# Gated cross-attention and FFN on one core: order of the first chunk, reciprocal in halves, a second buffer for the left-over values

## The chip, the cores and the metric

The kernel runs on one core of one Trainium2 chip. The metric is the device time of one execution in microseconds (us), lower is better. The engines are TensorE (PE: matmuls; PEld: its weight loads), VectorE (DVE), ScalarE (ACT), GpSimd (POOL) and SyncE (SP), which here only issues DMAs.

## The reference

Four batches of 2048 tokens with 512 features attend to 154 context rows each, then pass an FFN with a hidden layer of 2048. What is computed:

```python
x = x + tanh(g_xattn[0]) * xattn(layernorm(x), ctx)     # q, k, v, 16 heads of 32, softmax, Wo, bo
x = x + tanh(g_ffn[0]) * ffn(layernorm(x))
# ffn: h = relu(x @ w1.T + b1); hq, wq = fp8(4,3) of h and w2; out = fp16-like(hq @ wq.T + fp16-like(b2))
```

x is (4, 2048, 512) float32, w1 (2048, 512), w2 (512, 2048).

## The kernel before

The 8192 tokens are cut into 16 chunks of 512 tokens (4 tiles of 128). Four chunks belong to one batch. Products that need more than float16 are made of two float16 parts each (high and low) in three passes; the first chunk's q and all k and v are made in float32 directly. Every weight in parts is scaled by a power of two taken from its largest magnitude: `magnitude` reduces a weight to a column of `mag`, `fold` brings the columns together over the partitions, `powers` makes the scales.

The order of all work is written out by hand in **beats**. A chunk c starts at beat 28c; lists such as `VALUE_AT` or `O_AT` give the beats of each stage relative to that, and every engine runs the same loop over beats in its own program, calling the stages that are due. Engines meet through semaphores. Because stages reach from beat -40 to 69, chunk c's attention runs beside the projection, hidden layer and FFN output of chunk c-1. For chunk 0 there is no such work beside it.

Per chunk: `ln1_stat`/`ln1_apply` (VectorE), `x_hi` (ScalarE) and `x_lo` (GpSimd) split x, `turn_x` (SP, L299) transposes both parts by DMA into `xT`; `query` (PE), `query_out`, `query_hi`, `query_lo`; `q_stack` (SP, 12 DMAs a pair). `rank` (PE, L502) makes scores for the row maximum into `m_ps`, `row_max` (DVE, L861) reduces them; one `rank` waits for the `row_max` before it. `shift` and `shift_row` bring the maxima into the stacked q. `lift_left` and `lift_main` (PE) make the shifted scores in `s_ps`, `exps` (ACT) and `probs` (GpSimd) the probabilities in two parts. Of 154 context rows 128 are the main part; the left-over 26 of four heads are laid block by block into `vblk` (`values_diagonal`, SP, L356), once a batch. `value` (PE, L542) sums the probabilities into `d_ps` and the weighted values into `y_ps`; `normalise` (DVE, L878) takes the reciprocal of `d_ps` into `y32` and multiplies by `y_ps`. Then `project` (PE) with `residual` (DVE, with `resid` loaded again from x by `reload`, SP, and `add_bias`, GpSimd), `ln2_inverse` (GpSimd), `ln2_apply` (DVE, into `xn2`), `x2_hi`, `x2_lo`, `turn_x2` (SP, L307) into `late_a`, `hidden` and `relu`, `ffn_out` (PE, L591) and `finish` (DVE, L890: `ffn16`, then the sum into `resid`), `store`. The ring of two PSUM banks serves q, projection, hidden layer and FFN output in order; a job waits until the job two places before it has been read.

Each batch change (chunks 4, 8, 12) also loads `kblk` (`keys_diagonal`) and `kcat` (`keys_stacked`) anew, and `vblk`, which waits for the last `value` of the batch before, because there is one buffer:

```python
if b:
    sp.wait_ge(valued, b * CPB * KT)      # values_diagonal, VBLK_AT = [1]
...
nc.vector.reciprocal(y32[:], d_ps[:]).then_inc(inverted, 1)      # normalise, VALUE_AT
nc.vector.tensor_tensor(y32[:], y_ps[:], y32[:], ALU.mult).then_inc(y_scaled, 1)
```

The beginning (before the loop over beats) loads x, the context, wk, wv, wq and the small arrays on SP's queue, wo and three quarters of w1 on ScalarE's queue once x is turned (`move_turned`); VectorE makes the magnitudes and folds them (`kv_scales`), moves the first four k and v products, folds again with wq (`q_scales`) and moves the first q through the one buffer `q32`; ScalarE casts, GpSimd subtracts.

Of the kernel before, what the change touches and what calls it, by code (L numbers as in the profile page):

```python
# [25 lines left out]
STACK = 3  # L26
PASSES = ((0, 0), (0, 1), (1, 0))
# [5 lines left out]
Q_LOG, K_LOG = 10, 12  # L33

# [43 lines left out]
def build(nc, x, ctx_t, g_xattn, g_ffn, wq_t, bq, wk_t, bk, wv_t, bv, wo_t, bo, w1_t, b1, w2_t, b2, out):  # L78
# [10 lines left out]
    with ExitStack() as es:  # L89
# [17 lines left out]
        vblk = sb("vblk", [P, 2, KT, P], F16)  # L107
# [37 lines left out]
        fold_b = sb("fold_b", [P, 8], F32)  # L145
        amax = sb("amax", [P, 32], F32)
# [65 lines left out]
        kv_done, kv_moved, kv_hi, kv_lo = sem("kv_done"), sem("kv_moved"), sem("kv_hi"), sem("kv_lo")  # L212
        wo_hi_done, wo_ready, w1_hi, w1_ready, w2_ready = (
# [7 lines left out]
        def run(stage_fn, at, b):  # L221

            for k, r in enumerate(at):
                c, rest = divmod(b - r, PERIOD)
                if rest == 0 and 0 <= c < NCH:
                    stage_fn(c, k)

# [41 lines left out]

        def kv32(n):  # L270
            return kv_stage[:, n % 2 * C:(n % 2 + 1) * C]
# [19 lines left out]
        def _(sp):  # L291
# [7 lines left out]
            def turn_x(c, t):  # L299
                sp.wait_ge(x_split, (c - 1) * TILES + t + 1)  # L300
                if t == 0:
                    sp.wait_ge(q_done, c * KT)
                for part in range(2):
# [3 lines left out]
            def turn_x2(c, t):  # L307
                sp.wait_ge(x2_split, c * TILES + t + 1)
# [4 lines left out]
                for part in range(2):  # L313
# [24 lines left out]
            def keys_diagonal(b, k):  # L338
                if b:
                    sp.wait_ge(scored, b * CPB * 16)  # L340
                else:
                    sp.wait_ge(kv_hi, KT)
                    sp.wait_ge(cleared, 1)
# [12 lines left out]
            def values_diagonal(b, k):  # L356
                if b:
                    sp.wait_ge(valued, b * CPB * KT)
                else:
                    sp.wait_ge(kv_lo, KT + 1)  # L360
                for h in range(GH):
                    for a in range(2):
                        sp.dma_start(vblk[DH * h:DH * h + LEFT, a, :, DH * h:DH * h + DH],  # L363
# [41 lines left out]
            for beat in range(FIRST, (NCH - 1) * PERIOD + LAST):  # L405
                run(shift_row, SHIFT_AT, beat)
                run(lambda c, t: x_load(c, t) if c > 1 else None, XLOAD_AT, beat)
                run(turn_x2, X2TURN_AT, beat)
                run(lambda c, t: turn_x(c, t) if c else None, XTURN_AT, beat)
# [13 lines left out]
        def _(pe):  # L423
# [118 lines left out]
            def value(c, m):  # L542
                g, b = group(c, m), c // CPB
                pe.wait_ge(prob_lo, unit(c, m, GH) + 1)
                if g:
                    pe.wait_ge(inverted, g)
# [13 lines left out]
                if g:  # L560
                    pe.wait_ge(y_scaled, g)
                for p, (a, q) in enumerate(PASSES):
# [4 lines left out]
                    for h in range(GH):  # L567
                        last = pe.matmul(y_ps[DH * h:DH * h + DH, :], vblk[:, a, m, DH * h:DH * h + DH],  # L568
# [32 lines left out]

            for n in range(KT):
                turn(n)
# [4 lines left out]
            for beat in range(FIRST, (NCH - 1) * PERIOD + LAST):  # L608
# [3 lines left out]
                run(rank, MAX_AT, beat)  # L612
# [7 lines left out]
        def _(act):  # L620
# [13 lines left out]
            def wq_hi_part():  # L634
# [15 lines left out]
            def first_keys_stacked(pair):  # L650
                act.wait_ge(cleared, 1)
# [59 lines left out]
            def query_hi(c, m):  # L711
# [18 lines left out]
            nc.scalar.activation(sc[:, 8:10], gates[:], ACT.Tanh).then_inc(gate_done, 1)  # L730
            for n in range(KT):
# [4 lines left out]
            wq_hi_part()  # L736
            first_keys_stacked(1)
            w1_load(2)
            for beat in range(FIRST, (NCH - 1) * PERIOD + LAST):
# [7 lines left out]
                run(lambda c, t: x_hi(c, t) if c else None, XSPLIT_AT, beat)  # L747
                once(wo_hi, WO_HI, beat)
# [4 lines left out]
        def _(dve):  # L753
# [11 lines left out]
            def fold():  # L765

                link(nc.vector.transpose(fold_a[:], mag[:]))
# [53 lines left out]
            def o_w1_scales(n):  # L821
                fold()
                powers(pw[:, 3:8], rp[:, 3:8], amax[:, 7:12])
                dve.wait_ge(gate_done, 1)
                nc.vector.tensor_scalar(sc[:, 10:11], rp[:, 3:4], 2.0 ** 7, None, ALU.mult)
# [299 lines left out]
```

## Time and profile before

| what | value |
|---|---|
| time, median of 3 runs | 1725.39 us (1722.44 to 1725.61) |
| the profiled execution | 1727.09 us, its span 1725.3 us |
| PE busy | 1590.5 us, 92% |
| VectorE busy | 935.5 us, 54% |
| GpSimd busy | 864.4 us, 50% |
| ScalarE busy | 804.5 us, 47% |
| mean granted clock of PE | 0.966 |
| DMA, 127.3 MB | 74 GB/s on average |

The profile comes from one execution. The page cuts the span into 40 slices: PE's busy digit is 6, 6, 7, 5, 6 in the first five and mostly 9 after that, and the granted clock (PEclk, 1.0 is 2.4 GHz) shows an 8 and a 6 among the first five slices and a 9 or 8 later. The chain that ended last is PE for 74%, VectorE for 13% and SP's queue for 5%.

### The profile page before, as it was taken

What the parts mean: (1) busy time and instruction counts of PE and PEld (TensorE: products, weight loads), DVE (VectorE), ACT (ScalarE), POOL (GpSimd) and SP (SyncE); (2) the same over time, 40 slices, a digit from 0 to 9 for tenths busy, and PEclk for the clock granted to TensorE, in tenths of its full rate; (3) what the DMA queues carried; (4) which work ended last, traced back from release to release, by engine and by line L of the source; (5) the groups of instructions that cost most, each with busy time, mean ns of one, the idle gap of its engine ahead of it and who ended that gap; (6) DMA issues with size and microseconds to landing.
All of it is one profiled execution on the core that took longest, in us unless ns stands there. A gap on an engine that the chain in (4) does not pass through costs nothing.

```text
span 1725.3 us, 24606 instructions
## 1 busy us (share of the span) xinstructions
PE 1590.5 (92%) x9320; PEld 719.0 (42%) x9320; DVE 935.5 (54%) x1190; ACT 804.5 (47%) x1177; POOL 864.4 (50%) x918
## 2 busy tenths in 40 slices
PE   6675699999899999999979999999979999999998
PEld 3231244444334444444434444444434444444443
DVE  7767557464355746464554746455554645646131
ACT  1354563544345355444525545454534545453511
POOL 2457556473444647364444736465453646535420
PEclk9896899999999999999989999999999999999999
DMA  7322243132222313233231323323232322222010
GB/s 276 76 73 73 68 116 99 36 79 80 68 74 60 101 33 82 71 77 79 63 92 32 81 74 74 74 74 83 53 67 73 77 70 75 56 62 74 0 50 25
DMA packets 216293, 127.30 MB, mean 74 GB/s; under 512 B 164976, under 2 KB 189552, under 8 KB 214512
## 3 DMA queue, kind: packets, MB, share of 16 engines
q1 hardware_dynamic: 213536, 120.01, 27.1%
q10 hardware_dynamic: 2640, 5.72, 0.9%
q8 instruction: 74, 1.21, 0.3%
q14 instruction: 43, 0.35, 0.1%
HBM read 48.20 MB, written 16.78 MB: 38 GB/s over the span
## 4 chain that ended last, share of the span: by engine, by line
PE 74%; DVE 13%; SPq 5%; issue 4%; POOL 2%; DMA 1%; ACT 1%; ACTq 0%; DVEq 0%
PE ring L428 47%; PE ring L598 14%; DVE y L885 3%; PE m_ps L512 3%; PE s_ps L539 2%; PE y_ps L565 2%; DVE resid L925 2%; PE y_ps L568 2%; DVE bns L908 2%; DVE smax L865 2%; PE d_ps L554 1%; SPq L363 1%; SPq L354 1%; PE d_ps L557 1%; SPq L304 1%
## 5 line engine op out<-in xcount | busy, mean ns | idle before, releaser
L428 PE MATMUL ring<-late_a,w 128*128 128x512 f16 x3072 | 698.5, 380 | 9.1 <-DMA late_a<-x 9.1
L428 PEld LDWEIGHTS ring<-late_a,w 128*128 128x128 f16 x3072 | 297.7, 98 | 361.1 <-issue 25.0
L1001 POOL TENSOR_TENSOR pmain<-p,pmain 128x512 f16<-128x512 f32 x256 | 302.7, 1184 | 157.4 <-ACT p L673 155.7
L694 ACT ACTIVATE late_b<-ring,b_sb,wsc 128x512 fp8e4<-128x512 f32 x256 | 199.1, 778 | 349.9 <-PE ring L428 349.7
L865 DVE TENSOR_REDUCE smax<-m_ps 128x4 f32<-128x616 f32 x256 | 202.8, 792 | 221.3 <-PE m_ps L512 220.9
L885 DVE RECIPROCAL y<-d_ps 128x512 f32<-128x512 f32 x64 | 214.6, 3353 | 99.4 <-PE d_ps L557 99.4
L673 ACT ACTIVATE p<-s_ps,prob_log,sc 128x512 f32<-128x512 f32 x320 | 247.2, 773 | 1.2 <-POOL pmain L1001 1.2
L598 PE MATMUL ring<-w,late_b 128*128 128x512 fp8e4 x1024 | 239.9, 393 | 1.5 <-ACT late_b L694 0.9
L1001 POOL TENSOR_TENSOR pleft<-p,pleft 128x512 f16<-128x512 f32 x64 | 74.8, 1168 | 280.3 <-ACT p L673 280.3
L670 ACT ACTIVATE pmain<-s_ps,prob_log,sc 128x512 f16<-128x512 f32 x256 | 197.9, 773 | 15.2 <-PE s_ps L539 15.1
L428 PE MATMUL ring<-wo,yT 128*128 128x512 f16 x768 | 177.7, 382 | 0.0
L512 PE MATMUL m_ps<-kblk,qparts 128*128 128x308 f16 x512 | 112.5, 302 | 69.3 <-DVE smax L865 65.9
L428 PE MATMUL ring<-xT,wq 128*128 128x512 f16 x720 | 165.1, 379 | 0.5 <-DVE x L843 0.5
L709 ACT CAST x<-xn 128x512 f16<-128x512 f32 x64 | 39.6, 618 | 270.1 <-DVE xn L934 270.1
L598 PEld LDWEIGHTS ring<-w,late_b 128*128 128x128 fp8e4 x1024 | 103.0, 101 | 129.7 <-issue 16.8
L1013 POOL TENSOR_TENSOR qparts<-q,qparts 128x512 f16<-128x512 f32 x64 | 74.0, 1156 | 121.5 <-ACT qparts L716 121.5
L904 DVE TENSOR_SCALAR q<-ring,sc,bias_s 128x512 f32<-128x512 f32 x62 | 50.2, 809 | 139.6 <-PE ring L428 136.3
L1027 POOL TENSOR_TENSOR x<-xn,x 128x512 f16<-128x512 f32 x64 | 79.7, 1246 | 72.9 <-ACT x L709 72.9
L894 DVE TENSOR_TENSOR ffn<-ring,bq 128x512 f16<-128x512 f32 x64 | 44.1, 689 | 124.8 <-PE ring L598 123.9
L918 DVE TENSOR_SCALAR xin<-xin,mv,rs 128x512 f32<-128x512 f32 x64 | 49.9, 780 | 113.6 <-POOL rs L1039 113.5
L428 PEld LDWEIGHTS ring<-wo,yT 128*128 128x128 f16 x768 | 75.6, 98 | 82.4 <-issue 2.8
L512 PEld LDWEIGHTS m_ps<-kblk,qparts 128*128 128x128 f16 x512 | 44.8, 98 | 150.7 <-issue 105.9
(131 smaller groups left out, 1594.5 us busy)
## 6 DMA issues: line engine op xcount, KB each, us to landing
qstack<-qparts SPq DMA_DIRECT2D x384, 64.0 KB, 2.0
xin<-in_x SPq DMA_DIRECT2D x64, 256.0 KB, 3.5
resid<-in_x SPq DMA_DIRECT2D x64, 256.0 KB, 3.0
out_x<-resid SPq DMA_DIRECT2D x64, 256.0 KB, 2.3
resid<-in_w_t SPq DMA_DIRECT2D x4, 1024.0 KB, 5.0
qstack<-negT SPq DMA_DIRECT2D x128, 2.0 KB, 1.7
late_a<-x SPq DMA_TRANSPOSE x128, 2.5
xT<-x SPq DMA_TRANSPOSE x120, 2.5
```

The lines of the kernel that those rows point to most:

```text
L428: last = pe.matmul(dst, lhs(a, k), rhs(b, k), start=(k == 0 and p == 0), stop=(k == n_k - 1 and p == 2))
L512: last = pe.matmul(m_ps[:, half, 0:HK], qparts[:, 0, m, t * P:t * P + P], kblk[:, m, half * HK:(half + 1) * HK], start=True, stop=True)
L598: last = pe.matmul(ring_bank("f", c, t)[:], hT[:, j, t * P:t * P + P], w2[:, j, :], start=(j == 0), stop=(j == HT - 1))
L670: nc.scalar.activation(dst, s_ps[n % 2][:], ACT.Exp, bias=prob_log[:, 0:1], scale=sc[:, 7:8])
L673: nc.scalar.activation(p32[:, n % 2, :], s_ps[n % 2][:], ACT.Exp, bias=prob_log[:, 0:1], scale=sc[:, 7:8]).then_inc(exped, 1)
L694: nc.scalar.activation(hT[:, j, :], ring_bank("h", c, j)[:], ACT.Relu, bias=b1_sb[:, j:j + 1], scale=wsc[:, j // 4, 1:2], saturate=False). ...
L865: nc.vector.tensor_reduce(smax[:, heads, t].rearrange("p (a h) -> p a h", a=2), score_view, AX.X, ALU.max).then_inc(maxed, 1)
L885: nc.vector.reciprocal(y32[:], d_ps[:]).then_inc(inverted, 1)
L904: nc.vector.tensor_scalar(q32[:], ring_bank("q", c, m)[:], sc[:, 6:7] if c else sc[:, 5:6], bias_s[:, m:m + 1], ALU.mult, ALU.add).then_in ...
L1001: nc.gpsimd.tensor_tensor(part[:, 1, :], p32[:, n % 2, :], part[:, 0, :], ALU.subtract).then_inc(prob_lo, 1)
L1013: nc.gpsimd.tensor_tensor(qparts[:, 1, m, :], q32[:], qparts[:, 0, m, :], ALU.subtract).then_inc(q_lo, 1)
L1027: nc.gpsimd.tensor_tensor(x2_16[:, t % 2, 1, :], xn2[:], x2_16[:, t % 2, 0, :], ALU.subtract).then_inc(x2_split, 1)
```

## The change

- `vblk` gets a second buffer, chosen by b % 2; `values_diagonal` moves from beat 1 to beat -24 of the batch's first chunk and waits only for the values of the batch before the last.
- `normalise` works on halves of 256 columns, one in beat 7, 14, 21, 28 and one in the beat after (`NORMAL_AT`). `inverted` and `y_scaled` count two a group; their readers wait for both.
- `turn_x` and `turn_x2` wait for the high part, issue its transpose, then wait for the low part; SP's loop calls `turn_x2` ahead of `shift_row`.
- Beginning: PE turns all of x ahead of the key products; wq's magnitude comes into the first fold, the second fold goes; the magnitudes for wo and w1 become sums of magnitudes (`ACT.Abs` with `accum_out` into `sums`) on ScalarE, four of them ahead of the first key casts, the fifth (w1 part 2) at beat 9; the scale uses `W_LOG` = 13 in place of 7. wq's split moves to beats 0 (high) and 6 (low), the load of w1 part 2 to beat 7, the splits of w1 to beats 18 to 23 and 39, 40 (before 20, 21, 27, 28, 32, 33, 37, 38).
- The first q is staged in four buffers (`p32` twice, `q32`, `y32`), so `query_out` doesn't wait between them; the second half of chunk 0's row maxima runs at beats -2 to 5 (before 2 to 9).
- `kcat`'s and `ones_left`'s clearing moves from GpSimd to the start of VectorE's program; `cleared` counts two.

```diff
+FIRST_MAX_AT = [-10, -9, -8, -7, -6, -5, -4, -3, -2, -1, 0, 1, 2, 3, 4, 5]
+FIRST_SHIFT_AT = [-3, 5]
-VBLK_AT = [1]
+VBLK_AT = [-24]
+NORMAL_AT = [7, 8, 14, 15, 21, 22, 28, 29]
-WO_MAG = {0: -1}
-W1_MAG = {0: 0, 1: 1, 3: 8, 2: 9}
+WQ_HI, WQ_LO = {0: 0}, {0: 6}
+W1_LATE = {2: 7}
+W1_SUM = {2: 9}
-W1_HI = {1: 20, 2: 27, 0: 32, 3: 37}
-W1_LO = {1: 21, 2: 28, 0: 33, 3: 38}
+W1_HI = {1: 18, 2: 20, 0: 22, 3: 39}
+W1_LO = {1: 19, 2: 21, 0: 23, 3: 40}
...
+        def q_stage(c, m):
+            if c:
+                return q32[:]
+            return (p32[:, 0, :], p32[:, 1, :], q32[:], y32[:])[m]
...
             def turn_x2(c, t):
-                sp.wait_ge(x2_split, c * TILES + t + 1)
...
-                for part in range(2):
+                for part, split in enumerate((x2_hi_done, x2_split)):
+                    sp.wait_ge(split, c * TILES + t + 1)
                     sp.dma_start_transpose(x2T[:, part, :, t * P:t * P + P], x2_16[:, t % 2, part, :]
                                            ).then_inc(x2t_in[t % 2], DMA)
...
             def values_diagonal(b, k):
-                if b:
-                    sp.wait_ge(valued, b * CPB * KT)
-                else:
+                if b > 1:
+                    sp.wait_ge(valued, (b - 1) * CPB * KT)
+                if b == 0:
                     sp.wait_ge(kv_lo, KT + 1)
...
+            def magnitudes(n):
+
+                act.wait_ge(w_in["wo"] if n == 4 else w1_in[n], DMA)
+                if n < 4:
+                    act.wait_ge(summed, (1, 2, 4, 3)[n])
+                nc.scalar.activation(flat(wo[:, 1]), wo_raw if n == 4 else w1_stage[n], ACT.Abs,
+                                     accum_out=sums[:, n:n + 1]).then_inc(summed, 1)
...
             nc.scalar.activation(sc[:, 8:10], gates[:], ACT.Tanh).then_inc(gate_done, 1)
+            act.wait_ge(cleared, 2)
+            magnitudes(4)
+            for n in (0, 1, 3):
+                magnitudes(n)
             for n in range(KT):
                 keys_values(n)
             first_keys_stacked(0)
...
-            def normalise(c, m):
-                g = group(c, m)
-                dve.wait_ge(den_done, g + 1)
-                if g:
-                    dve.wait_ge(y_lo_done, g)
-                else:
-                    dve.wait_ge(chain, steps[0])
-                nc.vector.reciprocal(y32[:], d_ps[:]).then_inc(inverted, 1)
-                dve.wait_ge(inverted, g + 1)
+            def normalise(c, k):
+                m, half = divmod(k, 2)
+                g, cols = group(c, m), slice(half * HALF_COLS, (half + 1) * HALF_COLS)
+                if half == 0:
+                    dve.wait_ge(den_done, g + 1)
+                    if g:
+                        dve.wait_ge(y_lo_done, g)
+                    else:
+                        dve.wait_ge(q_lo, KT)
+                nc.vector.reciprocal(y32[:, cols], d_ps[:, cols]).then_inc(inverted, 1)
+                dve.wait_ge(inverted, 2 * g + half + 1)
                 dve.wait_ge(valued, g + 1)
-                nc.vector.tensor_tensor(y32[:], y_ps[:], y32[:], ALU.mult).then_inc(y_scaled, 1)
+                nc.vector.tensor_tensor(y32[:, cols], y_ps[:, cols], y32[:, cols], ALU.mult).then_inc(y_scaled, 1)
...
-            query_out(0, 2)
-            query_out(0, 3)
-            lo_of(wq_raw, flat(wq[:, 0]), flat(wq[:, 1]), sc[:, 2:3], wq_hi, 1, wq_ready)
+            for m in range(KT):
+                query_out(0, m)
```

## Rows read from the trace of the kernel before

**Rows 1.** Windows: us, busy us of each engine (x count), PEclk, DMA share, GB/s

```profile
0.00:195.40 195.40, 120.27 (x560) 53.69 (x560) 140.56 (x212) 77.34 (x110) 100.96 (x117) 0.83 0.39 117
195.40:1600.00 1404.60, 1351.86 (x8154) 612.63 (x8155) 766.01 (x942) 691.09 (x1017) 737.83 (x774) 0.98 0.29 72
```

**Rows 2.** Waits, 300 to 1600 us: total us, times, longest us

```profile
PE m_ps L512 <- DVE smax L865: 33.2, 19, 3.5
...
PE d_ps L554 <- DMA vblk<-vleft: 17.6, 3, 6.2
```

**Rows 3.** PE's timeline: start us, us, what [idle before <- releaser]

```profile
278.77 0.42 PE L512 MATMUL m_ps<-kblk,qparts 128*128 128x308 f16 x2 [1.95 <-DVE smax L865]
...
374.98 0.42 PE L512 MATMUL m_ps<-kblk,qparts 128*128 128x308 f16 x2 [1.95 <-DVE smax L865]
...
582.37 0.42 PE L512 MATMUL m_ps<-kblk,qparts 128*128 128x308 f16 x2 [1.95 <-DVE smax L865]
...
667.82 0.40 PE L554 MATMUL d_ps<-pmain,ones 128*32 128x512 f16 x4
...
678.59 0.42 PE L512 MATMUL m_ps<-kblk,qparts 128*128 128x308 f16 x2 [1.95 <-DVE smax L865]
...
686.20 7.07 PE L598 MATMUL ring<-w,late_b 128*128 128x512 fp8e4 x32
...
1573.07 0.42 PE L512 MATMUL m_ps<-kblk,qparts 128*128 128x308 f16 x2 [1.83 <-DVE smax L865]
```

**Rows 4.** PE's timeline at the first change of batch

```profile
468.20 0.62 PE L554 MATMUL d_ps<-pmain,ones 128*32 128x512 f16 x4 [6.01 <-DMA vblk<-vleft]
...
483.50 0.67 PE L512 MATMUL m_ps<-kblk,qparts 128*128 128x308 f16 x2 [3.50 <-DVE smax L865]
```

**Rows 5.** VectorE's timeline in an ordinary chunk

```profile
671.62 3.35 DVE L885 RECIPROCAL y<-d_ps 128x512 f32<-128x512 f32 x1
675.00 0.69 DVE L888 TENSOR_TENSOR y<-y_ps,y 128x512 f32<-128x512 f32 x1
675.61 0.54 DVE L934 TENSOR_SCALAR xn<-resid,mv,rs 128x512 f32<-128x512 f32 x1
...
677.67 0.77 DVE L865 TENSOR_REDUCE smax<-m_ps 128x4 f32<-128x616 f32 x1
678.98 1.37 DVE L934 TENSOR_SCALAR xn<-resid,mv,rs 128x512 f32<-128x512 f32 x1 [0.54 <-POOL rs L1039]
...
684.46 0.68 DVE L894 TENSOR_TENSOR ffn<-ring,bq 128x512 f16<-128x512 f32 x1
```

**Rows 6.** Timelines of SP and VectorE at the first change of batch

```profile
459.73 7.06 SPq L363 DMA_DIRECT2D vblk<-vleft  x8
466.84 0.99 SPq L374 DMA_DIRECT2D resid<-in_x  x2
...
473.04 1.30 DVE L934 TENSOR_SCALAR xn<-resid,mv,rs 128x512 f32<-128x512 f32 x1
```

**Rows 7.** The small reciprocals of L783: ns min/median/max, first and last start

```profile
L783 DVE RECIPROCAL rp<-pw x3: 165/166/190, 23.5 to 105.2; 128x1 f32<-128x1 f32 x1, 128x2 f32<-128x2 f32 x1, 128x5 f32<-128x5 f32 x1
```

**Rows 8.** DMA issues (KB, us to landing) and timelines of the beginning

```profile
w<-in_w_t ACTq DMA_DIRECT2D x1, 1024.0 KB, 15.0
...
28.17 8.03 ACTq L654 DMA_DIRECT2D kcat<-kst  x12
...
52.13 0.67 PE L512 MATMUL m_ps<-kblk,qparts 128*128 128x308 f16 x2 [6.44 <-DVE smax L865]
...
77.65 7.02 SPq L363 DMA_DIRECT2D vblk<-vleft  x8
...
100.11 2.28 DVE L763 TENSOR_REDUCE mag<-late_a 128x1 f32<-128x2048 f32 x1
...
168.98 2.34 DVE L787 SCALAR_TENSOR_TENSOR w<-late_b,wsc,w 128x2048 f16<-128x2048 f32 x1
...
195.45 4.37 PE L428 MATMUL ring<-late_a,w 128*128 128x512 f16 x12 [9.13 <-DMA late_a<-x]
```

More of the change, by code:

```diff
@@ L299, in turn_x @@
             def turn_x(c, t):
-                sp.wait_ge(x_split, (c - 1) * TILES + t + 1)
                 if t == 0:
                     sp.wait_ge(q_done, c * KT)
-                for part in range(2):
+                for part, split in enumerate((x_hi_done, x_split)):
+                    sp.wait_ge(split, (c - 1) * TILES + t + 1)
                     sp.dma_start_transpose(xT[:, part, :, t * P:t * P + P], x16[:, t % 2, part, :]
@@ L567, in value @@
                     for h in range(GH):
-                        last = pe.matmul(y_ps[DH * h:DH * h + DH, :], vblk[:, a, m, DH * h:DH * h + DH],
+                        last = pe.matmul(y_ps[DH * h:DH * h + DH, :], vblk[:, b % 2, a, m, DH * h:DH * h + DH],
                                          pleft[:, g % 2, q, :], start=False, stop=(p == 2))
@@ L600, in ffn_out @@
                 last.then_inc(ffn_done, 1)
+            for t in range(TILES):
+                turn(t)
             for n in range(KT):
-                turn(n)
                 for k in range(KT):
@@ L747, in _ @@
                 run(lambda c, t: x_hi(c, t) if c else None, XSPLIT_AT, beat)
+                once(wq_hi_part, WQ_HI, beat)
+                once(w1_load, W1_LATE, beat)
+                once(magnitudes, W1_SUM, beat)
                 once(wo_hi, WO_HI, beat)
@@ L763, in magnitude, with fold @@
                 link(nc.vector.tensor_reduce(mag[:, col:col + 1], src, AX.X, ALU.max, apply_absolute_value=True))
-            def fold():
-                link(nc.vector.transpose(fold_a[:], mag[:]))
+            def fold(columns):
+                link(nc.vector.transpose(fold_a[:], columns[:]))
                 link(nc.vector.tensor_reduce(fold_b[:, 0:1], fold_a[:], AX.X, ALU.max))
@@ L937, in _ @@
             nc.vector.memset(prob_log[:], PROB_LOG)
-            link(nc.vector.memset(mag[:], 0.0))
+            nc.vector.memset(mag[:], 0.0)
+            nc.vector.memset(sums[:], 0.0)
+            nc.vector.memset(kcat[0:97, :, P:KW], 0.0)
+            link(nc.vector.memset(ones_left[:], 0.0))
+            nc.vector.memset(kcat[96:97, :, 0:NK], SHIFT).then_inc(cleared, 1)
+            for h in range(GH):
+                nc.vector.memset(ones_left[DH * h:DH * h + LEFT, DH * h:DH * h + DH], 1.0)
             for t in range(TILES + 1):
@@ L948, in _ @@
                 magnitude(2 + n, src)
+            dve.wait_ge(w_in["wq"], DMA)
+            magnitude(0, wq_raw)
             dve.wait_ge(w_in["bias"], 2 * DMA)
@@ L953, in _ @@
             magnitude(6, bv32)
-            fold()
+            fold(mag)
             kv_scales()
+            q_scales()
             for n in range(KT):
                 keys_values(n)
-            dve.wait_ge(w_in["wq"], DMA)
-            magnitude(0, wq_raw)
-            fold()
-            q_scales()
-            dve.wait_ge(cleared, 1)
-            for h in range(GH):
-                nc.vector.memset(ones_left[DH * h:DH * h + LEFT, DH * h:DH * h + DH], 1.0)
-            nc.vector.memset(kcat[96:97, :, 0:NK], SHIFT)
-            query_out(0, 0)
-            query_out(0, 1)
             dve.wait_ge(gate_done, 1)
@@ L984, in _ @@
                 run(lambda c, t: ln1_apply(c, t) if c else None, LN1_APPLY_AT, beat)
-                once(wo_mag, WO_MAG, beat)
-                once(w1_mag, W1_MAG, beat)
+                once(wq_lo, WQ_LO, beat)
                 once(o_w1_scales, W_FOLD, beat)
@@ L1056, in _ @@
             nc.gpsimd.memset(kblk[:].rearrange("p m n -> p (m n)").bitcast(F32), 0.0)
-            nc.gpsimd.memset(kcat[:, :, P:KW], 0.0)
-            nc.gpsimd.memset(vblk[:].rearrange("p a m n -> p (a m n)").bitcast(F32), 0.0)
-            nc.gpsimd.memset(ones_left[:].bitcast(F32), 0.0)
+            nc.gpsimd.memset(vblk[:].rearrange("p b a m n -> p (b a m n)").bitcast(F32), 0.0)
             nc.gpsimd.memset(ones[:], 1.0).then_inc(cleared, 1)
```

68 lines of the change are left out of this document (35 added, 33 removed).

## The prediction

> **What bounds the kernel now.** I cut the span first into three stretches. From 195.4 to 1600 us TensorE (PE) is busy 1351.9 of 1404.6 us at a granted clock of 0.98; from 0 to 195.4 us it is busy 120.3 of 195.4 us at 0.83; the last 125.3 us hold 118.3 us of PE work at full clock [rows 1]. So the middle is PE's own work plus few stalls, the beginning is a chain of latencies, and the tail has next to nothing to give.
>
> The waits of the middle say what the stalls are: PE waited 33.2 us, in 19 waits, for VectorE's row maxima (`m_ps` <- `smax`), and 17.6 us, in 3 waits, for the DMA of `vblk` [rows 2]. PE's timeline then gives the pattern. An undisturbed chunk is 96.22 us (582.37 to 678.59), and has exactly one stall, 1.95 us, before the last row-maximum matmul (beat 9) [rows 3]. At a change of batch there is the big one: 6.01 us for `vblk` at 468.20, then 3.50 us at 483.50; the two periods from 374.98 to 582.37 take 207.39 us instead of 2 x 96.22 = 192.44, so 15.0 us are lost there, more than the stalls' sum, since the matmuls behind them are slow (`d_ps` 0.62 us for four against 0.40) [rows 3, 4]. From 278.77 to 1573.07 there are 13 periods in 1294.30 us, and 13 x 96.22 = 1250.9: **43.4 us** are lost to three batch changes and their slow clock [rows 3].
>
> VectorE's own timeline shows why the 1.95 us stall is there: RECIPROCAL 3.35 us at 671.62 and the product 0.69 us stand in one piece between two row maxima, and the next maximum starts at 677.67 [rows 5].
>
> **The change, part by part.** *Two buffers for `vblk`.* Now SP issues the eight copies at 459.73 for 7.06 us, because they wait for the last value of the old batch, and the `resid` loads of that chunk come only behind them, at 466.84; VectorE's chain (`xn`, 473.04) starts when these have landed [rows 6]. With two buffers the copies go 25 beats earlier and wait for nothing that is still running. The beat they go to has on SP two transposes and then a gap; I count at most 1 us of delay there, hidden, since the transposes of x2 end some us before PE wants them. The `vblk` wait goes whole. What is late next are the `resid` loads: they move up by the 7.06 us of SP's copies, so `xn` starts at about 466.0. From 473.04 to the stalled matmul at 483.50 were 10.5 us [rows 4, 6]; less 1.95 for the halved reciprocal (below) that is 8.5, so the matmul stands at 474.5. Undisturbed, it would come as far behind the value matmuls as in an ordinary chunk: 462.2 (468.20 less 6.01) + 10.77 (678.59 less 667.82) - 1.9 = 471.0 [rows 3, 4]. So 3.5 us stay, and 0.8 more for the next link of the same chain: 4.3 us a change of batch. Part: -43.4 + 3 x 4.3 = **-30.5 us**. Bounds: -43.4 (nothing stays) and -15 (the stall moves to `resid` nearly whole, with its slow clock).
>
> *Reciprocal in halves.* Each normalise becomes two pieces in two beats, and a row maximum can stand between them. One column costs 165 ns, 512 cost 3349 [rows 5, 7]: 6.2 ns a column, so 256 cost 1.76 us; the product of a half is 0.37 to 0.45 by the same reasoning. A half is 2.15 us, two are 4.3 against 4.05: +0.25 us of VectorE each, and the first piece is 1.9 us shorter than the whole. The row maximum that now starts at 677.67 can start 1.9 us earlier, which is the whole 1.95 us stall. But VectorE has the same work up to `ffn16` at 684.46 (end 685.15), and that frees the bank for the third FFN product, which PE starts at 686.20 [rows 3, 5]: only 1.05 us of margin. PE can gain at most 1.05 us there, plus what VectorE's chain itself shortens: the 0.54 us in which it waited for GpSimd's deviation (before `xn` at 678.98) is now filled by the second half, less the 0.25 added. 1.05 + 0.54 - 0.25 = 1.3 us a chunk, 14 chunks (278.77 to 1573.07): **-18.2 us**. Bounds: 14 x 1.95 = -27.3, and +3 if a port conflict eats it. A half does not delay its reader: the value matmuls of the next group come seven beats later, and the cast of y two beats later.
>
> The same `xn` operation takes 0.54 us at 675.61 and 1.37 us at 678.98, where GpSimd was working [rows 5]. The Trainium skill ("SBUF — State Buffer", "SBUF: two separate sides") says that an instruction of VectorE in a two-port mode and one of GpSimd exclude each other for their whole length; the trace agrees (0.83 us more). By this rule the first `xn`, moved forward by 1.9 us, can fall onto GpSimd's subtraction of `pleft` and cost 0.83 us: the gain would be 0.5 us a chunk, 7 us in all. I keep that in the range.
>
> *The transposes of x and x2 wait for each part alone, and x2's go ahead of the shift rows.* SP issues the high part while GpSimd computes the low one, 1.25 us earlier. In the middle PE never waits for them; at the first FFN it does (below).
>
> *The beginning.* (a) The three loads of w1 and that of wo start some 10 us earlier, as PE now turns all of x first. But ScalarE now sums the magnitudes of wo and three w1 parts ahead of the first keys, in program order, so it waits for the last of these loads. That load took 15.0 us from 24.56, to 39.6 [rows 8]. Between 24 and 38 us the DMA engines are full, before they have some 2 us to spare, so it lands at about 37.5, and with 2.0 us of sum the first key cast goes from 25.35 to about 39.5. Behind it stand the key stacking on ScalarE's queue (8.03 us [rows 8]) and the casts of q, so the first row maximum moves from 40.74 to 51 or 52. That is where the second stands today, 52.13, as VectorE is at wq until then [rows 8]; from there they follow each other as now. Cost: 0 to +2, I take **+1.5**. (b) SP's stacking and the eight `vblk` copies (77.65 to 84.67) release the first values at 85.92 [rows 8]; they stay as they are, so the four sums of magnitude taken off VectorE around 68 to 77 us (2.28 us each) buy nothing. Those at 96 and 100 us are on the path to the fold and wo: the fold now waits for the w1 part loaded at beat 7 (5.1 us to land, as the page has it, and 2.0 to sum), so of 4.6 us some 2.8 are won: **-2.8**. (c) The w1 splits leave beats 27 to 33 (VectorE 2.34 us at 168.98, in front of a row maximum [rows 8]) for beats 18 to 23, where VectorE has idle pieces: **-2.3**. (d) Transposes: -1.25 by the split parts behind the shift at 143, and at 188.96 four transposes in a row stood behind the shift row; now two of them have gone already, and the first FFN product, which waited 9.13 us until 195.45, starts 2.5 earlier [rows 8]: **-3.7**. Sum +1.5 - 2.8 - 2.3 - 3.7 = **-7.3 us**. Bounds: +10 (ScalarE's wait for the loads and a slow clock carried through), -25 (the idle part of PE in this stretch is 75 us; a third of it).
>
> *Nothing:* the memsets that go from GpSimd to VectorE (2.11 us of `kcat`) stand before the first x lands at 3.57 us; the doubled memset of `vblk` is behind nobody. wq's split moves to beats 0 and 6, which is 2.35 us on VectorE before the values; `vblk` covers it.
>
> **Sum.** -30.5 - 18.2 - 7.3 = -56.0 us. The profiled execution took 1727.09 us; -56.0 gives 1671.1. The median of the runs, 1725.39, is 1.7 us lower: 1669.4, rounded **1670 us**.
>
> **The rivals.**
> 1. *All stalls go* (chance 0.17): the `resid` loads land in time, VectorE's chain loses its waits, the beginning runs on without its w1 splits: -43.4 - 27.3 - 18 = -88.7, **1637 us**. For it: PE is at 96% of the middle and each part removed is a real wait. Against: VectorE's 1.05 us of margin.
> 2. *VectorE's chain takes the place of what is removed* (0.22): the halves give 0.5 us a chunk, each change of batch keeps 9 us (`resid` behind `kcat` on SP), the beginning nothing: -7 - 43.4 + 27 = -23.4, **1702 us**. For it: two thirds of the batch's loss come behind the `vblk` wait.
> 3. *The beginning turns worse* (0.08): ScalarE is held until 39.5, PE idles and resumes at the slow level, and 15 us come on top: -48.7 + 15, **1692 us**.
> 4. *Slower* (0.04): a half reciprocal costs almost what a whole one does, 3.35 us more per normalise; in the stretch from 671 to 685 that is on PE's path once a chunk, with the second normalise's half perhaps twice. It would be slower from 3.5 us a chunk on (56 over 16); at 2 x 3.35 us it is 107 - 56 = +51, **1776 us**. Against it: one, two and five columns take 165 to 190 ns [rows 7].
> 5. *It doesn't do what it says* (0.02): the copies of `vblk` still wait behind something on SP; within 0.2% of before only if the halves give nothing either.
> My own case has the other 0.47.
>
> **Numbers.** The likeliest is 1670. Range 1642 to 1702: rival 3 and nearly all of rival 2 are in, most of rival 1 is left out below and rivals 4 and 5 above. No change means within 0.2% (3.5 us), about what the measurement of this kernel can tell. Faster 0.94, the same 0.02, slower 0.04.
>
> **What would show it.** Right: no wait of PE for `vblk`; the eight copies in the middle of the last chunk of a batch; ordinary periods of about 94.9 us; a maximum at beat 9 without stall but the third FFN product waiting some tenths for `ffn16`; at a change of batch 3 to 5 us of `m_ps` <- `smax`, led back to `resid`; 128 reciprocals of 1.76 us; the first key cast near 39 us; the first FFN product near 188 us. Wrong: halves over 2 us; periods of 96; waits of 8 us and more at a change of batch; a first FFN product after 195.

## The result, and the profile after

| | before | after |
|---|---|---|
| median | 1725.39 us | 1682.92 us (4 runs, 1682.06 to 1685.74) |
| span of the profiled execution | 1725.3 us | 1681.9 us |
| PE busy, mean granted clock | 1590.5 us, 0.966 | 1576.8 us, 0.977 |

The ratio is 0.9761 with a 95% interval of 0.9744 to 0.9777: faster by 2.4%. The forecast was 1670, range 1642 to 1702.

The page of the profile after, its head and sections 1 and 2:

```profile
span 1681.9 us, 24791 instructions
PE 1576.8 (94%) x9320; PEld 715.2 (43%) x9320; DVE 942.3 (56%) x1305; ACT 812.9 (48%) x1187; POOL 867.1 (52%) x916
PE   4775699999999999999989999999989999999998
PEclk8996899999999999999999999999999999999999
```

The waits of PE from 300 to 1600 us (engine, tile and line, releaser: us in total, times, longest), against [rows 2]:

```profile
PE d_ps L574 <- POOL pmain L1029: 13.4, 4, 4.1
PE m_ps L532 <- DVE smax L894: 10.6, 12, 2.1
```

The 17.6 us for `vblk` are gone and those for the row maxima fell from 33.2 to 10.6, but a wait that was not there before has come: the value matmuls for GpSimd's `pmain`. PE's timeline of an ordinary chunk, of the first FFN product and of the first change of batch (start, us, what, idle before and its releaser), against [rows 3, 4]:

```profile
193.20 4.20 PE L448 MATMUL ring<-late_a,w 128*128 128x512 f16 x12 [7.00 <-DMA late_a<-x]
274.93 0.42 PE L532 MATMUL m_ps<-kblk,qparts 128*128 128x308 f16 x2 [0.53 <-DVE smax L894]
...
459.36 0.62 PE L574 MATMUL d_ps<-pmain,ones 128*32 128x512 f16 x4 [4.11 <-POOL pmain L1029]
...
471.71 0.42 PE L532 MATMUL m_ps<-kblk,qparts 128*128 128x308 f16 x2 [2.05 <-DVE smax L894]
...
568.18 0.43 PE L532 MATMUL m_ps<-kblk,qparts 128*128 128x308 f16 x2 [0.53 <-DVE smax L894]
...
662.98 0.42 PE L532 MATMUL m_ps<-kblk,qparts 128*128 128x308 f16 x2 [0.54 <-DVE smax L894]
...
670.59 7.07 PE L618 MATMUL ring<-w,late_b 128*128 128x512 fp8e4 x32
...
1435.40 0.43 PE L532 MATMUL m_ps<-kblk,qparts 128*128 128x308 f16 x2 [0.54 <-DVE smax L894]
```

The reader is to see three things. The ordinary period is 662.98 - 568.18 = 94.80 us, 1.42 less than 96.22. With one more such period the last row maximum's matmul of chunk 15 would stand at 1435.40 + 94.80 = 1530.20, so 13 periods take 1255.27 us; 13 x 94.80 = 1232.4, and **22.9 us** are still lost, all at the three changes of batch, where before 43.4 us were lost in all [rows 3]. Of these 43.4 only 36.7 belong to the changes: behind four ordinary stalls of 1.95 us (those that end at 374.98, 774.80, 1174.07 and 1379.07) the next 16 FFN matmuls took 5.30 us in place of 3.62, at a granted clock of 0.68, which is 4 x 1.68 = 6.7 us. And the first FFN product is only 2.25 us earlier than in [rows 8]. The whole difference of the spans adds up: beginning -2.25; from there to the matmul of chunk 2 -1.59 (81.73 for 83.32); the 13 periods -18.5 by the shorter period and -20.5 by what is lost less (-13.8 at the changes of batch, -6.7 behind ordinary stalls); the rest -0.6, which is the last period (94.23 us, as its stall is missing); together -43.4.

The first of the four in the kernel before, behind the stall that ended at 374.98 [rows 3]:

```profile
375.25 5.30 PE L598 MATMUL ring<-w,late_b 128*128 128x512 fp8e4 x16
```

The queue behind the new wait, SP's timeline at the first change of batch, and GpSimd's:

```profile
441.81 7.64 SPq L374 DMA_DIRECT2D kcat<-kst  x12
449.49 0.59 SPq L394 DMA_DIRECT2D resid<-in_x  x1
450.13 2.53 SPq L324 DMA_TRANSPOSE xT<-x  x2
452.71 1.54 SPq L394 DMA_DIRECT2D resid<-in_x  x3
```

```profile
452.53 1.27 POOL L1061 TENSOR_TENSOR resid<-resid,gbo 128x512 f32<-128x512 f32 x1 [7.49 <-DMA resid<-in_x]
453.75 1.15 POOL L1029 TENSOR_TENSOR pmain<-p,pmain 128x512 f16<-128x512 f32 x1
455.82 1.26 POOL L1061 TENSOR_TENSOR resid<-resid,gbo 128x512 f32<-128x512 f32 x1 [0.92 <-DMA resid<-in_x]
...
458.15 1.15 POOL L1029 TENSOR_TENSOR pmain<-p,pmain 128x512 f16<-128x512 f32 x1
```

SP issues the 12 copies of the second half of the new batch's key stacking in 7.64 us; the loads of `resid` stand behind them. GpSimd's `add_bias` waits 7.49 us for the first of these, and GpSimd's queue being in order, the `pmain` subtractions behind it wait too. The last of them ends at 459.30, and the value matmuls start at 459.36.

### The profile page after: what moved, and what is told of

Same layout as the page of the kernel before. It is cut to its first block, busy times and chain, and to the rows that moved or that the text cites. A ratio compares the mean times of both kernels' runs of the same rounds, so it can differ in the third digit from the quotient of the medians.

```text
span 1681.9 us, 24791 instructions
## 1 busy us (share of the span) xinstructions
PE 1576.8 (94%) x9320; PEld 715.2 (43%) x9320; DVE 942.3 (56%) x1305; ACT 812.9 (48%) x1187; POOL 867.1 (52%) x916
## 4 chain that ended last, share of the span: by engine, by line
PE 69%; DVE 11%; SPq 8%; issue 4%; POOL 3%; DMA 3%; ACT 2%; ACTq 1%; DVEq 0%
PE ring L448 44%; PE ring L618 13%; PE m_ps L532 3%; SPq L347 3%; DVE y L916 2%; PE s_ps L559 2%; PE y_ps L588 2%; PE y_ps L585 2%; SPq L324 2%; DVE resid L956 2%; DVE bns L939 2%; DVE smax L894 2%; PE d_ps L574 1%; SPq L374 1%; DMA y<-in_b 1%
## 5 line engine op out<-in xcount | busy, mean ns | idle before, releaser
L916 DVE RECIPROCAL y<-d_ps 128x256 f32<-128x256 f32 x128 | 223.9, 1749 | 94.0 <-PE d_ps L577 94.0
L618 PE MATMUL ring<-w,late_b 128*128 128x512 fp8e4 x1024 | 229.9, 381 | 1.5 <-ACT late_b L723 0.9
L1041 POOL TENSOR_TENSOR qparts<-q,qparts 128x512 f16<-128x512 f32 x61 | 70.6, 1158 | 109.6 <-ACT qparts L745 109.6
L559 PE MATMUL s_ps<-qstack,kcat 97*128 97x512 f16 x256 | 98.2, 385 | 12.0 <-ACT p L702 11.8
L448 PEld LDWEIGHTS ring<-xT,wq 128*128 128x128 f16 x720 | 70.2, 98 | 78.0 <-issue 0.6
```

Of the source, the lines that this page charges most:

```text
L448: last = pe.matmul(dst, lhs(a, k), rhs(b, k), start=(k == 0 and p == 0), stop=(k == n_k - 1 and p == 2))
L559: pe.matmul(s_ps[unit(c, m, 1 + h) % 2][:], kcat[0:97, GH * m + h, 0:P], qstack[0:97, GH * m + h, :], start=True, stop=True).then_inc(lift ...
L618: last = pe.matmul(ring_bank("f", c, t)[:], hT[:, j, t * P:t * P + P], w2[:, j, :], start=(j == 0), stop=(j == HT - 1))
L916: nc.vector.reciprocal(y32[:, cols], d_ps[:, cols]).then_inc(inverted, 1)
L1041: nc.gpsimd.tensor_tensor(qparts[:, 1, m, :], q_stage(c, m), qparts[:, 0, m, :], ALU.subtract).then_inc(q_lo, 1)
```

## The experiments

One table for all; *lost* is the time between the last row-maximum matmuls of chunks 2 and 15 less 13 ordinary periods (96.22 us with the whole reciprocal, 94.80 with halves), read in each trace as above. *At changes* is this without the slow stretches behind ordinary stalls, 1.68 us each. Before, measured beside them, had medians of 1723.74 to 1725.22.

| kernel | median (range) | ratio to before, 95% | lost | at changes |
|---|---|---|---|---|
| before | 1725.39 (1722.44 to 1725.61) | 1 | 43.4 | 36.7 |
| after | 1682.92 (1682.06 to 1685.74) | 0.9744 to 0.9777 | 22.9 | 22.9 |
| two_buffers | 1713.42 (1710.65 to 1713.81) | 0.9921 to 0.9945 | 27.6 | 20.9 |
| halves | 1700.09 (1699.52 to 1701.25) | 0.9849 to 0.9874 | 36.8 | 36.8 |
| beginning_only | 1722.29 (1719.88 to 1726.69) | 0.9984 to 1.0003 | 40.2 | 35.2 |
| kcat_late | 1662.78 (1659.35 to 1664.05) | 0.9625 to 0.9651 | 0.0 | 0.0 |
| before_kcat | 1701.23 (1700.34 to 1704.69) | 0.9859 to 0.9886 | 19.4 | 14.4 |
| kcat_whole | 1690.52 (1688.92 to 1691.34) | 0.9792 to 0.9819 | 6.6 | 0 |
| sums_late | 1682.67 (1681.60 to 1685.33) | 0.9740 to 0.9766 | | |
| old_w1_beats | 1682.87 (1681.97 to 1683.66) | 0.9739 to 0.9766 | | |
| old_turns | 1688.82 (1685.60 to 1690.78) | 0.9772 to 0.9799 | 23.5 | 23.5 |
| kcat_sums | 1661.31 (1659.71 to 1663.84) | 0.9616 to 0.9642 | | |
| small_left | 1656.45 (1655.39 to 1658.06) | 0.9598 to 0.9624 | | |
| split_early | 1654.92 (1652.97 to 1656.61) | 0.9587 to 0.9613 | | |

**The three parts, each alone.** `two_buffers` is the kernel before with this:

```diff
-VBLK_AT = [1]
+VBLK_AT = [-24]
-vblk = sb("vblk", [P, 2, KT, P], F16)
+vblk = sb("vblk", [P, 2, 2, KT, P], F16)      # the buffer is b % 2
-                if b:
-                    sp.wait_ge(valued, b * CPB * KT)
+                if b > 1:
+                    sp.wait_ge(valued, (b - 1) * CPB * KT)
```

> The kernel before with the second vblk buffer and the copies at beat -24 alone. My theory: at a change of batch the value matmuls then wait for GpSimd's probabilities, which stand behind the addition of the bias to a late resid load (about 4 us of wait in place of 6), and the ordinary periods stay at 96.2 us with one stall of 1.95. In the changed kernel 22.9 us are left of the 43.4 that batch changes cost; here some 2 us more a change, as the whole reciprocal stands in VectorE's chain: -14 to -20 us, about 1708. Rival, each part pays for itself whatever else is there: -20.5 us with 1705 and no difference in the chain. Rival, VectorE's chain takes over what the copies free: under -8 us, over 1717.

It gave 11.3 us. PE's wait for `vblk` went and waits for GpSimd came in its place, of 3.57, 2.21 and 3.27 us; the first of them:

```profile
464.38 0.62 PE L554 MATMUL d_ps<-pmain,ones 128*32 128x512 f16 x4 [3.57 <-POOL pmain L1001]
```

`halves` is the kernel before with `normalise` in halves and the counts of its readers doubled:

```diff
+NORMAL_AT = [7, 8, 14, 15, 21, 22, 28, 29]
-                nc.vector.reciprocal(y32[:], d_ps[:]).then_inc(inverted, 1)
+                nc.vector.reciprocal(y32[:, cols], d_ps[:, cols]).then_inc(inverted, 1)
```

> The kernel before with the reciprocal in halves alone. My theory: the ordinary period goes from 96.22 to about 94.8 us (the stall of 1.95 us shrinks to 0.54, since one xn meets GpSimd's port), at the batch changes the 3.50 us stall shrinks too: 13 or 14 times 1.4 and some us, -20 to -24 us, about 1703. The beginning moves by under 2 us. Rival (my prediction's reason): the third FFN product waits for ffn16 and takes back the rest; then PE shows waits before L598 by VectorE. Rival, VectorE is only loaded more: no gain, 1725.

It gave 24.6 us. Its ordinary period is 94.80 us (574.90 to 669.69), so 1.42 x 14 = 19.9 of it are the ordinary chunks. The lost time went from 43.4 to 36.8, but not at the changes of batch: there the stall before the last maximum went from 3.50 to 2.08, while the three waits for `vblk` grew from 6.01, 5.33 and 6.24 us to 6.76, 5.80 and 6.50. What went are the slow stretches behind four ordinary stalls: behind a stall of 0.54 us there is none.

`beginning_only` is the kernel after with one `vblk` buffer at beat 1 and the whole reciprocal, that is, both edits above taken back.

> The changed kernel with one vblk buffer (beat 1) and the whole reciprocal: the beginning, the order of the transposes and the staged q are left. My theory: the first FFN product comes 1 to 3 us before 195.45 and the middle stays as it was, -1 to -4 us, about 1723. Rival, the beginning won its 7 us and the middle lost some of them: the first FFN product near 188 us and periods over 96.2. Rival, the beginning is a loss that the halves made up for: over 1727.

Its median is 2.4 us under that of before, measured beside it, 1724.72, and the interval holds 1: the beginning is worth about two microseconds or nothing. The three alone add up to 38.3 us; all together gave 42.5. Each of these has an interval of about 2 us to either side, so the difference isn't shown to be more than scatter.

**Where the rest of the batch's loss is.** `kcat_late` is the kernel after with one number changed:

```diff
-KST_AT = [-16, -2]
+KST_AT = [-16, 5]
```

> The changed kernel with the second stacking of keys (12 DMAs, 7.64 us of SP's queue at a change of batch) moved from beat -2 to beat 5, behind the resid loads. My theory: the loads land in time, GpSimd's additions and probabilities are not held, the waits of 4.1, 3.7 and 4.1 us for pmain go and so do the 1.9 to 2.05 us ones down to 0.54; of 22.9 us lost at three changes 15 to 22 come back: 1661 to 1668. Rival, the value matmuls wait because GpSimd itself is behind (its busy share is the highest at these chunks): under 3 us of gain, over 1680. Rival, the stacking then delays the transposes of x2 at beats 7 to 10 and hidden waits: a new wait of PE for late_a of some us at each change, gain under 8 us, 1675.

20.1 us less than after. Its waits of PE from 300 to 1600 us, and SP's timeline at the first change of batch:

```profile
PE m_ps L532 <- DVE smax L894: 6.4, 12, 0.5
PE d_ps L574 <- POOL pmain L1029: 1.5, 1, 1.5
```

```profile
444.37 0.59 SPq L394 DMA_DIRECT2D resid<-in_x  x1
445.02 2.53 SPq L324 DMA_TRANSPOSE xT<-x  x2
447.59 1.53 SPq L394 DMA_DIRECT2D resid<-in_x  x3
450.35 3.62 SPq L324 DMA_TRANSPOSE xT<-x  x2
454.01 8.41 SPq L374 DMA_DIRECT2D kcat<-kst  x12
```

A change of batch now costs nothing at all: from 277.46 to 1415.09 are twelve periods of 94.80 us. The one wait for GpSimd that is left lies in the last chunk.

So what was the wait for `vblk` in the kernel before? `before_kcat` is that kernel with the same one number changed, and nothing else.

> The kernel before with one edit: the second half of the next batch's key stacking (12 DMAs on SP, 7.6 us) goes from beat -2 to beat 5. Theory: in the kernel before this queue was not what ended the wait; the eight vblk copies wait for the last value of the old batch whatever stands ahead of them, so PE's wait for vblk stays at 5.3 to 6.2 us and the time is 1722 to 1726, no change. The move pays only once vblk has two buffers (there it gave 20 us). Rival: the key stacking had its own price before as well, in the 3.5 us stall behind the vblk wait: then 5 to 10 us less, 1715 to 1720.

I expected no change, and it is 22.5 us faster: my theory of the kernel before fell, and the rival was too small as well. PE's waits and SP's timeline of `before_kcat`:

```profile
PE m_ps L512 <- DVE smax L865: 31.8, 17, 3.5
PE d_ps L554 <- POOL pmain L1001: 1.5, 1, 1.5
```

```profile
446.87 0.59 SPq L374 DMA_DIRECT2D resid<-in_x  x1
447.50 2.52 SPq L304 DMA_TRANSPOSE xT<-x  x2
450.07 0.57 SPq L374 DMA_DIRECT2D resid<-in_x  x1
450.68 7.45 SPq L363 DMA_DIRECT2D vblk<-vleft  x8
```

No wait for `vblk` is left between 300 and 1600 us, with one buffer and the copies still at beat 1. The last values of the old batch had ended by 441.6 us (the row below), and the copies were issued at 459.73 [rows 6]: they did not wait for these values, but for their turn in SP's queue, where 12 copies of q (8.55 us from 439.30) and the 12 of the keys stood ahead of them. The trace of before shows it, SP's and PE's timelines there:

```profile
447.90 7.96 SPq L354 DMA_DIRECT2D kcat<-kst  x12
455.91 0.59 SPq L374 DMA_DIRECT2D resid<-in_x  x1
...
459.11 0.58 SPq L374 DMA_DIRECT2D resid<-in_x  x1
```

```profile
441.15 0.39 PE L568 MATMUL y_ps<-pleft,vblk 128*32 128x512 f16 x4
```

The second buffer does not become useless by this: in `before_kcat` the eight `vblk` copies, 7.45 us, still stand ahead of the last two `resid` loads, a stall of 3.50 us at the last maximum stays at each change, and 14.4 us are lost there. With the buffer as well (`kcat_whole`, next) nothing is lost at the changes.

`kcat_whole` is kcat_late with the whole reciprocal.

> kcat_late (two vblk buffers, key stacking at beat 5) with the reciprocal whole again. It measures the halves where a change of batch costs nothing. Theory: the halves are worth the shorter ordinary period, 96.22 against 94.80 us, 14 times 1.42 = 19.9 us, and nothing else, since no batch stall is left for them to shorten: 1682 to 1685. Rival: their gain on the kernel before (24.6 us) is what they are worth here too, as it lies in the clock that stays up with the stalls gone: 1686 to 1689.

Against kcat_late it is 27.7 us slower (28.8 by the ratios to the before that was measured beside each), more than both had it; the theory, that the shorter period is all, is out, and the rival's reason, the clock, is in the trace. Nine of its 13 periods are 96.22 us (the last of them 96.10); four are 97.90, and this is where they are longer, its PE timeline behind the stall of 1.95 us in an ordinary chunk and in one of the four, and the windows of these FFN products (window, us, busy us of the engines, PEclk, DMA share, GB/s):

```profile
470.14 3.62 PE L618 MATMUL ring<-w,late_b 128*128 128x512 fp8e4 x16
...
566.35 5.30 PE L618 MATMUL ring<-w,late_b 128*128 128x512 fp8e4 x16
```

```profile
566.35:571.65 5.30, 5.30 (x19) 2.09 (x17) 4.95 (x8) 2.47 (x4) 4.12 (x6) 0.68 0.44 52
470.14:473.76 3.62, 3.62 (x19) 1.67 (x17) 3.42 (x5) 2.09 (x4) 2.53 (x4) 1.00 0.40 81
```

The same 16 matmuls take 1.68 us longer at a granted clock of 0.68, partly at the lower level of 1.2 GHz. This happened behind four of the thirteen stalls of 1.95 us, and behind none of the thirteen of 0.54 us in kcat_late. So the halves are worth 14 x 1.42 = 19.9 us, 4 x 1.68 = 6.7 for the clock, and 1 to 2 that are in the scatter. The same holds over all traces: 18 of 53 ordinary stalls of 1.95 us in the five kernels with the whole reciprocal have the slow stretch behind them, and none of 76 of 0.38 to 0.59 us in seven kernels with halves. With the key copies moved, a change of batch costs nothing with the whole reciprocal either: its loss of 6.6 us is the four slow periods.

**What ends the ordinary chunk now.** `small_left` is kcat_late with part of one subtraction left out:

```diff
+                if c and (m, u) == (1, 0):
+                    nc.gpsimd.tensor_tensor(part[:, 1, 0:32], p32[:, n % 2, 0:32], part[:, 0, 0:32], ALU.subtract
+                                            ).then_inc(prob_lo, 1)
+                    return
```

> kcat_late with one GpSimd subtraction per chunk cut to 32 of its 512 columns (the low part of pleft of the second group, beat 7; from the second chunk on), so that part of the low parts is left out. That is the operation during which VectorE's xn takes 0.99 instead of 0.54 us, ahead of the last row maximum of the chunk. Theory (the two engines exclude each other for the length of the instruction): xn goes to 0.54, the stall of 0.54 us at the last maximum to about 0.1, the period from 94.80 to about 94.35, 13 to 14 times 0.45 = 6 us less than kcat_late's 1662.8: 1656 to 1658. Rival: xn's length has another cause, or ffn16 takes over as the wait of the third FFN product: period 94.7 to 94.8, 1661 to 1664.

`split_early` keeps all work, and moves one split out of the way:

```diff
-XSPLIT_AT = [-31, -28, -25, -22]
+XSPLIT_AT = [-31, -28, -25, -23]
```

> kcat_late with the split of the fourth x tile one beat earlier (XSPLIT_AT -23 instead of -22), all work kept. GpSimd's subtraction for it then stands in a gap of 1.01 us ahead of x2's low part, and the pleft subtraction is over by about 747.8 in the profile's time of an ordinary chunk, before xn starts at 748.03. Theory: xn goes from 0.99 to 0.54 us, period about 94.35 to 94.5, 4 to 6 us less than kcat_late: 1657 to 1659. Rival: the subtraction does not fit in the gap and pushes x2's low part and the deviation behind it, so the period stays at 94.8 or grows: 1662 to 1666.

The first held, with 6.3 us less than kcat_late, and the second gave more than expected, 7.9 (4.7 and 6.6 by the ratios to the before measured beside each): 14 x 0.44 = 6.2 are the period below, the rest lies in its beginning, which scatters by this much (below). GpSimd and VectorE in the kernel after:

```profile
659.11 1.16 POOL L1029 TENSOR_TENSOR pleft<-p,pleft 128x512 f16<-128x512 f32 x1
659.22 0.42 DVE L919 TENSOR_TENSOR y<-y_ps,y 128x256 f32<-128x256 f32 x1
659.56 0.99 DVE L965 TENSOR_SCALAR xn<-resid,mv,rs 128x512 f32<-128x512 f32 x1
```

and in `split_early`:

```profile
642.25 1.34 POOL L1050 TENSOR_TENSOR x<-xin,x 128x512 f16<-128x512 f32 x1
643.55 1.15 POOL L1055 TENSOR_TENSOR x<-xn,x 128x512 f16<-128x512 f32 x1
645.58 1.16 POOL L1029 TENSOR_TENSOR pleft<-p,pleft 128x512 f16<-128x512 f32 x1
646.90 0.54 DVE L965 TENSOR_SCALAR xn<-resid,mv,rs 128x512 f32<-128x512 f32 x1
```

In the first `xn` starts while `pleft` runs and ends 0.28 us after it (0.99 us); in the second `pleft` is over before `xn` starts (0.54 us). The period is 94.36 us (669.24 to 763.60 for the same matmul), 0.44 less, and the stall at the last maximum is gone. The other `xn` behave alike: in before and after together 37 of 128 began with no such GpSimd operation running and took 0.54 or 0.55 us; the other 91 began beside one and ended 0.27 to 0.29 us after it, however long that made them (0.78 to 1.49 us). This agrees with the Trainium skill ("SBUF — State Buffer", "SBUF: two separate sides"), by which the two engines hold the shared pair of ports for the whole of an instruction. From 190.96 to 1500 us PE is busy 1307.91 of 1309.04 us in `split_early`. It is the best version run: 4.0% under before, 28.0 us under after.

**The beginning.** `sums_late` is the kernel after with ScalarE's four sums behind the stacking of the first keys:

```diff
-            act.wait_ge(cleared, 2)
-            magnitudes(4)
-            for n in (0, 1, 3):
-                magnitudes(n)
...
             first_keys_stacked(1)
+            magnitudes(4)
+            for n in (0, 1, 3):
+                magnitudes(n)
```

> The changed kernel with ScalarE's four sums of magnitude (4 x 2.1 us) moved from ahead of the first key casts to behind the second stacking of keys. My theory: the first key cast comes at 32 us, when the last small array has landed, in place of 40.3; the 8.3 us travel through stacking and first q to the first left-over lift (69.56 to 62 to 64); then the sums hold ScalarE for 8 us near 52 to 60, which hides behind the row maxima. Some are lost at the fold, so the first FFN product comes 3 to 8 us earlier: 1675 to 1680. Rival, PE and SP set the pace there (the stacking of q, 7.65 us, and of vblk, 7.02 us): the lift comes earlier, but the first FFN product by under 2 us, 1681 or more.

No difference to after. The first key cast goes from 40.26 to 31.47 us, but the first left-over lift stands at 70.46, where it stood at 69.56: the early casts were on no one's path. ScalarE in the kernel after:

```profile
31.98 0.20 ACT L759 ACTIVATE sc<-gates 128x2 f32<-128x2 f32 x1 [17.75 <-DMA y<-in_b]
32.09 1.89 ACT L664 ACTIVATE wo<-resid 128x2048 f16<-128x2048 f32 x1
33.88 0.19 ACT L664 ACTIVATION_READ_ACCUMULATOR wo<-resid 128x1 f32 x1
...
40.26 0.78 ACT L648 CAST kst<-x 128x308 f16<-128x308 f32 x2
```

`kcat_sums` is kcat_late with the same move.

> The changed kernel with both the late second stacking of keys and the late sums. The two touch different stretches, so the gains of the two single runs should add: with my theories 1654 to 1663. Rival, they share SP's queue or the clock: over 1668.

1.5 us under kcat_late, with intervals that overlap (0.9616 to 0.9642, 0.9625 to 0.9651): not told apart.

`old_w1_beats` puts the splits of w1 back where they were:

```diff
-W1_HI = {1: 18, 2: 20, 0: 22, 3: 39}
-W1_LO = {1: 19, 2: 21, 0: 23, 3: 40}
+W1_HI = {1: 20, 2: 27, 0: 32, 3: 37}
+W1_LO = {1: 21, 2: 28, 0: 33, 3: 38}
```

> The changed kernel with the splits of w1 back at beats 20, 27, 32, 37 (high) and 21, 28, 33, 38 (low). My theory: the split at ScalarE's beat 22 (2.0 us at 135.4) and VectorE's at 128.8 (2.3 us) stand in the chain to the second shift row, so the old beats give the shift row 2 to 4 us earlier (145.5 to 142 or 143), and cost 2 us later at VectorE's 169: the first FFN product within 2 us of 193.2, the time 1681 to 1684. Rival (my prediction): the new beats win 2.3 us, so the old ones lose them: 195.5 and 1685 or more.

No difference in the medians, and the first FFN product is at 192.94 for 193.20 us. Counted from SP's first `vblk` copies the product comes after 112.56 us, where six kernels with the new beats (after, `beginning_only`, `kcat_late`, `kcat_whole`, `small_left`, `split_early`) need 113.84 to 114.87: in this stretch the new beats rather cost 1.3 to 2.3 us, which the medians do not show.

`old_turns` has both transposes wait for the low part, as before (`turn_x2` likewise), and `shift_row` ahead of `turn_x2`:

```diff
-                for part, split in enumerate((x_hi_done, x_split)):
-                    sp.wait_ge(split, (c - 1) * TILES + t + 1)
+                sp.wait_ge(x_split, (c - 1) * TILES + t + 1)
+                for part in range(2):
```

> The changed kernel with both transposes waiting for the low part and the shift row ahead of turn_x2 again. My theory: in the middle nothing changes (periods of 94.80); at the first FFN product the two transposes more behind the shift row cost 2 to 4 us, 193.2 to 195 or 197: 1685 to 1687. Rival, the split wait blocks SP as often as it helps (7.37 us for four transposes at 179.35): no difference, 1683. Rival, they matter at the batch changes too: 1690 and more.

5.9 us slower than after. Its first FFN product:

```profile
197.55 4.40 PE L448 MATMUL ring<-late_a,w 128*128 128x512 f16 x12 [9.12 <-DMA late_a<-x]
```

2.12 us are the wait itself, 9.12 for 7.00. The product is 4.35 us later altogether, but the six kernels with the new turns and the same beginning had it anywhere from 190.96 to 194.84. This scatter is there already at SP's first `vblk` copies (76.94 to 79.97, and 80.54 here). From these copies to the product it is 117.01 us here and 113.84 to 114.87 in the six: 2.1 to 3.2 us are the turns'. The chunks behind are as in after (lost 23.5 for 22.9), so what else is in the 5.9 us is not located.

## Why the forecast was right where it was

*Halves, -18.2 forecast.* Right in size for the period: -18.5 in the 13 periods, and some of the 1.6 before them. Left out were the 6.7 us of slow clock behind ordinary stalls, which the halves removed too (alone they gave 24.6). The reason given was not right. The 1.05 us of margin before the third FFN product did not bind: `ffn16` ended at 670.21 and the product started at 670.59, still 0.38 us of margin. What bound is the stall of 0.54 us that stayed at the last maximum, and 0.45 of this is `xn` against `pleft`, the conflict that the forecast had named and had priced at twice the size, as a bound. 1.95 - 0.53 = 1.42 came out beside 1.3 by two errors that met. The halves themselves are as worked out, 1.75 us forecast as 1.76 (duration ns min/median/max, first and last start):

```profile
L916 DVE RECIPROCAL y<-d_ps x128: 1745/1747/1759, 88.0 to 1584.4; 128x256 f32<-128x256 f32 x128
```

*Two buffers, -30.5 forecast, -20.5 measured, of which -13.8 at the changes.* The forecast put all of the 43.4 us on the changes of batch; 6.7 of them stood behind ordinary stalls and went with the halves. The mis-sized term is what is late next: 4.3 us a change were forecast to stay, 7.6 did. The forecast looked for it along VectorE's chain (`resid`, `xn`, last maximum) and had 3 to 5 us of `m_ps` <- `smax` there; that wait was 2.05 us. It did not follow GpSimd's queue, where `add_bias` for `resid` stands ahead of `pmain`: 4.11 us of wait, and the matmuls behind it slow (0.62 to 0.65 us for four, for 0.39). And it moved `resid` up by the copies' 7.06 us, but its sum left out what stood ahead of both in SP's queue, though its second rival named it (`resid` behind `kcat`). The deeper error is the sentence "because they wait for the last value of the old batch". They did not; a line of code that waits was taken for a wait that happened. `before_kcat` shows the price: one number that this change did not touch was worth 22.5 us by itself, twice the second buffer alone (11.3).

*Beginning, -7.3 forecast, -2.3 measured.* (a) The first key cast came at 40.26 (forecast 39.5), yet for another reason: ScalarE waited not for the last part of w1 but 17.75 us for the small arrays, whose last one took 22.2 us to land, behind the loads that now start earlier (13.1 before), and then took 8.3 us for four sums. The cost at the first values was 1.0 us (86.91 for 85.92; forecast 1.5), and `sums_late` shows that the cast was not its cause. (b) The fold starts 3.8 us earlier (98.65 for 102.42; forecast 2.8), but wo's high part only 1.5 (104.61 for 106.15): within the fold its four copies took 2.54 us for 0.95 and the scaling behind them 0.82 for 0.17, while GpSimd's subtractions ran. The shift row of the second chunk is 1.8 us later (145.51 for 143.71): the gain was handed back within 45 us. What takes the rest back is not isolated. (c) The w1 beats gave nothing, for -2.3. (d) The transposes gave -2.1 to -3.2, for -3.7: the one term that came near its forecast.

*The rivals.* The second, that VectorE's chain takes the place of what is removed, had the halves at 0.5 us and 9 us a change of batch; the changes came 1.4 us from its number and the halves at mine. The time lies between the two. That all stalls go (1637) did not come true here, nor in any run. But `kcat_late` and `split_early`, one and two numbers away, take the stalls of the middle away: 1654.9 is about that rival's time without the 18 us that it had for the beginning (1725.4 - 43.4 - 27.3 = 1654.7). VectorE did not stand against it. Half a reciprocal costs half.

## What to carry to other kernels

A wait in the profile names the transfer that came last; before giving the waiting thing a second buffer, ask of its issue when the condition it waits for was met, and what stood ahead of it in its queue. Here the condition had been met 18 us before, and moving twelve unrelated DMAs behind the urgent ones was worth twice the buffer. Where an in-order engine has one operation that waits for a DMA, everything behind it in that queue waits too: follow it on all engines, not only on the one that stalls today. And a stall can cost more than its length: behind a third of those of 1.95 us here the clock was lower.

## What the runs showed of the hardware

- The clock's share: behind 18 of 53 stalls of 1.95 us the next 16 FFN matmuls took 5.30 instead of 3.62 us (granted clock 0.68 for 1.00); behind stalls of 0.38 to 0.59 us, 76 of them, none did.
- A VectorE `tensor_scalar` on 512 float32 columns (`xn`) took 0.54 us by itself; begun beside a GpSimd subtraction or addition of two tensors it ended 0.27 to 0.29 us after that operation, in all 91 cases of before and after.
- A reciprocal in float32 goes by its columns: 165 ns at one, 1747 at 256, 3349 at 512.
- The 256 KB load of b2, issued on SP's queue, landed 22.2 instead of 13.1 us after its issue when four loads of 1 MB on ScalarE's queue began 4 us behind it instead of 13.
- ScalarE's sum of magnitudes, 2048 columns, is 1.9 us and 0.19 us for reading the accumulator, against 2.28 us of VectorE's reduction [rows 8].
